# Layer 0's probabilities turned by DMA in 16-bit planes, and a cross pair between layer 1's self pairs

## The chip, the cores and the metric

One core of one Trainium2 chip. The metric is the device time of one execution in microseconds, lower is better; the median of three runs of the kernel before is 4849.32 us (4847.84 to 4849.81).

## What is computed

Four transformer layers in a row over x of 32 batches x 112 tokens x 256 and a context of 32 x 375 x 256. Layers 0 and 2 have cross attention with 16 heads of 64 (layer 0 with 4 key and value heads), layers 1 and 3 self and cross attention with 16 heads of 16. The reference, cut to what matters:

```python
# layer 0: RMS norms, grouped cross attention, x + h @ wo.T
# layer 1: per attention
sim = einsum('bhid,bhjd->bhij', fq(q, dq, 128), fq(k, dk, 128)) * SCALE
attn = softmax(sim)
out = einsum('bhij,bhjd->bhid', fq(attn, dw, 0), fq(v, dv, 128)) @ wo + bo
# then a * gelu(g) @ ff_w2, with a, g the halves of h3 @ ff_w1 + ff_b1
# layer 2: cross attention (h = 16, d = 64) and a relu feed-forward
# layer 3: causal self attention, cross attention, relu feed-forward
```

fq rounds to 8-bit steps; layer 1 therefore holds scores' operands and probabilities exactly in bf16, the other layers compute in f32.

## The kernel before, in words

Two batches make a stream of N = 224 tokens; 16 streams go through each layer, activations transposed (features on partitions). An attention is cut into octets of 8 heads of one batch; two heads (units) make a pair. The order of pairs is written out in `place_attention`: a stream of layer 0 or 2 has 4 cross octets of 4 pairs; in layers 1 and 3 two octets of self pairs (2 pairs each, four heads per unit) stand inside the first two cross octets, after their second pair. So a layer 1 stream has 20 pairs.

A pair goes through: scores on PE into 2 of 4 PSUM banks (`tensor_scores`; scores of a pair wait for the exponentials of the pair two before, and in the layers of `QUADS` two pairs are issued together), max on VectorE (L1698), exp on ScalarE with a running sum (L1563), reciprocal on VectorE (L1705), weighing on GpSimd (L1961 in layer 1, L1964 in the others), into one of 8 slots of `e`. Then the probabilities must be transposed, in one of three ways:

- turn: PE transposes them (`tensor_turn`, L1380, three 112 x 125 chunks a unit) into a PSUM ring, ScalarE or VectorE copy to `probs` (L1603, L1784). Layers 0 and 3, and layer 3's self pairs (L1377).
- layer 1: VectorE writes bf16 steps (L1746), a DMA transpose from SyncE's queue puts them into `probs` (L2001).
- in words, for the layers of `WORDS` (layer 2's cross pairs): the f32 words are split into two planes of 16-bit halves (VectorE L1730 or GpSimd L1946, by pair in turn), SyncE issues a DMA transpose into `planes` (L1996, the flip), and VectorE (L1734) or ScalarE (L1537) merges the halves to f32 in `probs`. There are three slots for halves (`SPLITS`), two for planes (`PLANES`); a flip waits for the merge two pairs before.

The value products (L1411 in layer 0, L1418 in layer 2, L1426 in layer 1, L1401 for self) follow when an octet is turned. All projections (L1437) and norms go through the same ring of 4 PSUM banks as jobs, each with a save by VectorE or ScalarE. Layer 1's gate and up products (h by weights) end in a Gelu on ScalarE (L1531).

`Plan.arrange` lays all steps in a fixed order for each engine beforehand: from the steps' engines, costs and positions it takes for each free engine the ready step of lowest position; steps marked "VA" go to whichever of VectorE and ScalarE is free. The engines then run these orders with semaphores. A changed cost, engine or position so moves instructions everywhere.

```python
WORDS = (2,)
SPLIT_BY = ("V", "G")
QUADS = (0, 2, 3)
self.add("split", p, by, 1.7, p.index + 1.4)
self.add("flip", p, "D", 4.2, p.index + 1.6)
self.add("merge", p, "VA", 1.45, p.index + 2.4)
```

## Time and profile before

| | |
|---|---|
| median of 3 runs | 4849.32 us |
| profiled execution | 4847.86 us, span 4846.1 us |
| PE busy | 4440.9 us, 92% |
| VectorE / ScalarE / GpSimd busy | 2955.7 / 2974.7 / 2282.1 us |
| mean granted TensorE clock | 0.955 |
| layer 0, layer 1, layer 2, layer 3, roughly | to 921, 2216, 3690, 4846 us |

The page cuts the span into 40 slices of 121 us, with a digit for the busy tenths of each engine. Rows of groups give the count, busy time and mean of one instruction. Busy time of back-to-back instructions is counted once where they overlap. A 4-byte matmul shows as two records, a transpose as one.

### The profile page before, as it was taken

How to read it: one execution, taken by the hardware profiler on the slowest of the kernel's cores; microseconds unless marked ns; L12 is line 12 of the kernel's file. 1: busy time of each engine (PE TensorE's matmuls, PEld its weight loads, DVE VectorE, ACT ScalarE, POOL GpSimd, SP SyncE). 2: the span in 40 equal slices, each digit the busy share in tenths (PEclk: the TensorE clock that was granted, in tenths of full speed). 3: DMA queues.
4: the chain of work that ended last, by engine and by line, in shares of the span. 5: the costliest groups of instructions: out<-in, count | busy, mean ns of one | idle time of the engine just before them, and what ended most of it. 6: DMA issues, size and time to landing. Idle time of an engine off the chain costs nothing.

```text
span 4846.1 us, 84907 instructions
## 1 busy us (share of the span) xinstructions
PE 4440.9 (92%) x30496; PEld 3230.0 (67%) x30496; DVE 2955.7 (61%) x6426; ACT 2974.7 (61%) x9009; POOL 2282.1 (47%) x4132
## 2 busy tenths in 40 slices
PE   8999999967787878789999999999999999999998
PEld 5666666646565656566666666666667777778777
DVE  6566566566666666666555555555555666667665
ACT  4555555688888888885444454444445666666664
POOL 3333333465656565664444444444444444444443
PEclk9999999979888888889999999999999999999999
DMA  2000000032333232343433333333332100000000
GB/s 85 21 21 24 21 21 22 25 90 62 62 61 64 61 62 63 61 86 68 98 76 77 75 74 77 77 74 74 77 76 47 41 19 19 18 19 19 18 18 7
DMA packets 631891, 249.53 MB, mean 51 GB/s; under 512 B 596784, under 2 KB 613424, under 8 KB 630064
## 3 DMA queue, kind: packets, MB, share of 16 engines
q1 hardware_dynamic: 631472, 244.10, 23.0%
q8 instruction: 244, 4.00, 0.3%
q14 instruction: 175, 1.43, 0.1%
HBM read 82.53 MB, written 14.68 MB: 20 GB/s over the span
## 4 chain that ended last, share of the span: by engine, by line
PE 82%; ACT 8%; POOL 4%; DVE 3%; issue 2%; DMA 2%; SPq 0%; ACTq 0%; POOLq 0%; DVEq 0%
PE ring L1437 51%; PE score L1366 11%; PE ring L1380 7%; ACT e L1563 5%; PE ring L1418 3%; PE ring L1411 3%; PE ring L1426 2%; DMA probs<-halves 2%; POOL e L1961 1%; POOL e L1964 1%; PE ring L1377 1%; PE ring L1401 1%; ACT work L1624 1%; PE ring L1452 1%; DVE nmax L1698 1%
## 5 line engine op out<-in xcount | busy, mean ns | idle before, releaser
L1964 POOL TENSOR_SCALAR e<-e,rsum 112x375 f32<-112x375 f32 (+1 forms) x2048 | 1102.2, 556 | 1677.4 <-DVE rsum L1705 1642.5
L1698 DVE TENSOR_REDUCE nmax<-score 112x2 f32<-112x750 f32 (+1 forms) x1152 | 1066.4, 951 | 407.0 <-PE score L1366 406.4
L1563 ACT ACTIVATE e<-score,nmax 112x375 f32<-112x375 f32 (+1 forms) x2048 | 1038.6, 537 | 117.8 <-DVE nmax L1698 115.5
L1437 PE MATMUL ring<-h,weights 128*128 128x224 f32 x3840 | 872.1, 369 | 34.5 <-ACT work L1624 24.9
L1437 PEld LDWEIGHTS ring<-h,weights 128*128 128x128 f32 x3840 | 734.3, 197 | 145.1 <-issue 52.7
L1366 PE MATMUL score<-keys,q 64*112 64x375 f32 (+2 forms) x3584 | 607.3, 493 | 235.4 <-ACT e L1563 231.4
L1603 ACT COPY probs<-ring 125x336 f32<-125x336 f32 (+1 forms) x625 | 252.5, 452 | 746.2 <-PE ring L1380 635.4
L1366 PEld LDWEIGHTS score<-keys,q 64*112 64x112 f32 (+2 forms) x3584 | 232.7, 166 | 539.0 <-ACT e L1563 289.5
L1437 PE MATMUL ring<-weights,ctx 128*128 128x512 f32 (+4 forms) x1536 | 587.1, 515 | 0.0
L1437 PE MATMUL ring<-ctx,weights 128*128 128x375 f32 x1536 | 567.2, 491 | 1.0 <-DVE heads L1799 0.8
L1563 ACT ACTIVATE e<-score,nmaxc,quant 112x375 f32<-112x375 f32 (+1 forms) x1024 | 555.1, 554 | 10.7
L1961 POOL TENSOR_SCALAR e<-e,rsumw 112x375 f32<-112x375 f32 (+1 forms) x1024 | 497.2, 505 | 30.3
L1380 PEld LDWEIGHTS ring<-consts,e 112*125 112x125 f32 x3072 | 372.4, 188 | 129.3 <-issue 90.4
L1563 ACT ACTIVATION_READ_ACCUMULATOR e<-score,nmax 112x1 f32 x2048 | 458.1, 224 | 0.0
L1380 PE MATMUL ring<-consts,e 112*125 112x112 f32 x3072 | 415.3, 279 | 5.1 <-POOL e L1964 3.0
L1437 PEld LDWEIGHTS ring<-weights,ctx 128*128 128x128 f32 (+2 forms) x1536 | 306.9, 202 | 143.8 <-issue 96.2
L1437 PE MATMUL ring<-work,weights 128*128 128x224 f32 (+1 forms) x1792 | 398.4, 372 | 1.0 <-DVE work L1827 0.6
L1437 PEld LDWEIGHTS ring<-ctx,weights 128*128 128x128 f32 x1536 | 277.6, 191 | 174.6 <-issue 66.8
L1437 PEld LDWEIGHTS ring<-work,weights 128*128 128x128 f32 x1792 | 335.1, 190 | 38.6 <-issue 12.3
L1850 DVE COPY values<-ring 125x128 f32<-125x128 f32 (+4 forms) x368 | 162.3, 470 | 272.9 <-PE ring L1437 272.0
L1437 PE MATMUL ring<-heads,weights 128*128 128x224 f32 x1536 | 323.0, 359 | 3.6 <-ACT work L1624 1.8
L1437 PEld LDWEIGHTS ring<-heads,weights 128*128 128x128 f32 x1536 | 286.1, 192 | 21.3 <-issue 10.2
(128 smaller groups left out, 5782.1 us busy)
## 6 DMA issues: line engine op xcount, KB each, us to landing
ctx<-ctx_t SPq DMA_DIRECT2D x128, 375.0 KB, 3.1
out_t<-x SPq DMA_DIRECT2D x64, 224.0 KB, 2.0
x<-out_t SPq DMA_DIRECT2D x48, 224.0 KB, 2.6
weights<-weights SPq DMA_DIRECT2D x7, 1024.0 KB, 5.9
probs<-halves SPq DMA_TRANSPOSE x320, 2.7
planes<-halves SPq DMA_TRANSPOSE x256, 3.4
x<-x_t SPq DMA_DIRECT2D x16, 224.0 KB, 2.5
weights<-weights SPq DMA_DIRECT2D x1, 3328.0 KB, 11.5
```

The source lines that it names most:

```text
L1366: ins = pe.matmul(score_bank(u)[0:S, n * width:(n + 1) * width], lhs, rhs, start=not masked, stop=not masked or n == nt - 1)
L1380: ins = pe.transpose(dst[0:R, c * S:(c + 1) * S], src[:, c * R:(c + 1) * R], idt[0:S, 0:S])
L1411: ins = pe.matmul(ps[64 * odd:64 * odd + 64, 0:4 * S], vs[chunk_rows(0, c), c, kv:kv + 64], four_heads(o, c, odd), start=c == 0, stop=c == ...
L1418: ins = pe.matmul(ps[64 * odd:64 * odd + 64, i * S:(i + 1) * S], vs[chunk_rows(2, c), c, hd:hd + 64], probs_of(o, c, 2 * i + odd if plan.i ...
L1426: ins = pe.matmul(ps[32 * p:32 * p + 32, 0:S], vs[chunk_rows(layer, c), c, hd:hd + 32], probs_of(o, c, p + 4 * odd, S), start=c == 0 and o ...
L1437: ins = pe.matmul(out_, a, b_, start=n == 0, stop=n == len(parts) - 1)
L1563: ins = nc.scalar.activation(e_of(u)[:, n * width:(n + 1) * width], score_bank(u)[0:S, n * width:(n + 1) * width], ACT.Exp, bias=minus, sc ...
L1603: ins = nc.scalar.copy(dst, src)
L1698: ins = dve.tensor_reduce(to, src, AX, ALU.max, negate=True)
L1850: ins = dve.tensor_copy(dst, src)
L1961: ins = nc.gpsimd.tensor_scalar(mine, mine, rsumw[0:S, slot(u), n:n + 1], ROUND, ALU.mult, ALU.add)
L1964: ins = nc.gpsimd.tensor_scalar(mine, mine, rsum[0:S, slot(u), n:n + 1], 0.0, ALU.mult, ALU.add)
```

## The change

Cross pairs of layer 0 now go in words as layer 2's: `WORDS = (0, 2)`. The split is made in two instructions per pair, one per half plane: in layer 0 one on GpSimd and one on ScalarE (new for it), in layer 2 both on VectorE or both on GpSimd as before. All merges, of layer 2 too, are VectorE's. Layer 0 leaves `QUADS`: its scores are issued pair by pair. The chunks of layer 0's context become 128, 128 and 119 rows, as in layer 2. In layer 1, of the two self pairs of an octet one stands after the second and one after the third cross pair. Layer 0's output projections get a position one pair later. The slots of `halves` are shared with layer 1's steps by address. Planner costs follow.

```diff
-WORDS = (2,)
-SPLIT_BY = ("V", "G")
+WORDS = (0, 2)
+SPLIT_BY = {0: ("GA",), 2: ("VV", "GG")}
+MERGE_BY = "V"
...
-QUADS = (0, 2, 3)
+QUADS = (2, 3)
...
-                        if beside and n == 1:
+                        if beside and layer == 1:
+                            if n in (1, 2):
+                                self.pair(beside)
+                        elif beside and n == 1:
                             self.pair(beside)
                             self.pair(beside)
...
-        self.row(e + 3.5, e + 4.6, [("o", layer, s, 0, m, "V") for m in range(KC)])
+        late = 1.0 if layer == 0 else 0
+        self.row(e + 3.5 + late, e + 4.6 + late, [("o", layer, s, 0, m, "V") for m in range(KC)])
...
-                by = SPLIT_BY[self.nth_halved[p] % len(SPLIT_BY)]
-                self.add("split", p, by, 1.7, p.index + 1.4)
-                self.add("flip", p, "D", 4.2, p.index + 1.6)
-                self.add("merge", p, "VA", 1.45, p.index + 2.4)
+                by = SPLIT_BY[o_.layer]
+                for h in range(2):
+                    e = by[self.nth_halved[p] % len(by)][h]
+                    self.add("split", (p, h), e, {"G": 0.95, "A": 0.8, "V": 0.6}[e], p.index + 1.4)
+                self.add("flip", p, "D", 3.5, p.index + 1.6)
+                self.add("merge", p, MERGE_BY, 0.9 if MERGE_BY == "V" else 1.2, p.index + 2.4)
...
+                elif kind == "split":
+                    to, src = split(wait, *x_)
+                    nc.scalar.copy(to, src).then_inc(halved["A"], 1)
...
-            return [(to[:, h, :, 0:T], src[:, h, :, :]) for h in range(2)]
+            return to[:, h, :, 0:T], src[:, h, :, :]
```

How instructions move. PE in layer 0, the middle of a stream, before (consts by e are the transposes, heads by weights the output projection, h by weights the queries, work by weights the keys, probs by values the value products):

```order
L1366 MATMUL score<-keys,q 112x375 x4
L1380 MATMUL ring<-consts,e 125x112 x12
L1437 MATMUL ring<-heads,weights 128x224 x16
L1366 MATMUL score<-keys,q 112x375 x4
L1380 MATMUL ring<-consts,e 125x112 x12
L1437 MATMUL ring<-h,weights 128x224 x4
L1437 MATMUL ring<-work,weights 128x375 x2
L1411 MATMUL ring<-probs,values 64x448 x6
L1366 MATMUL score<-keys,q 112x375 x4
L1380 MATMUL ring<-consts,e 125x112 x12
```

and with the change, a like piece:

```order
L1378 MATMUL score<-keys,q 112x375 x2
L1423 MATMUL ring<-probs,values 64x448 x6
L1378 MATMUL score<-keys,q 112x375 x4
L1449 MATMUL ring<-heads,weights 128x224 x16
L1378 MATMUL score<-keys,q 112x375 x2
L1423 MATMUL ring<-probs,values 64x448 x6
L1378 MATMUL score<-keys,q 112x375 x2
L1449 MATMUL ring<-work,weights 128x375 x2
L1378 MATMUL score<-keys,q 112x375 x2
L1449 MATMUL ring<-h,weights 128x224 x2
L1378 MATMUL score<-keys,q 112x375 x2
```

The transposes are gone, and each pair's scores stand alone with other work between most of them.

ScalarE in layer 0, before (probs from ring are turn copies, e from score the exponentials):

```order
L1603 COPY probs<-ring 125x3x112 x3
L1563 ACTIVATE e,sums<-score,nmax 112x375 x4
L1603 COPY probs<-ring 125x3x112 x2
L1563 ACTIVATE e,sums<-score,nmax 112x375 x4
L1664 COPY keys<-ring 128x375
L1603 COPY probs<-ring 125x3x112 x2
L1563 ACTIVATE e,sums<-score,nmax 112x375 x4
```

and now:

```order
L1549 COPY halves<-e 112x2x375 x2
L1664 ACTIVATE q<-ring 128x224
L1578 ACTIVATE e,sums<-score,nmax 112x375 x2
L1664 ACTIVATE q<-ring 128x224
L1578 ACTIVATE e,sums<-score,nmax 112x375 x2
L1549 COPY halves<-e 112x2x375
L1664 ACTIVATE q<-ring 128x224
L1578 ACTIVATE e,sums<-score,nmax 112x375 x4
L1549 COPY halves<-e 112x2x375 x2
L1664 ACTIVATE q<-ring 128x224
L1549 COPY halves<-e 112x2x375
L1664 ACTIVATE q<-ring 128x224
```

Copies to halves have taken the place of turn copies, and queries' saves have come over from VectorE.

PE in layer 1 around the second self octet, before (keys alone 112x112 are self scores, keys with q cross scores, probs by own the self values):

```order
L1366 MATMUL score<-keys 112x112 x8
L1437 MATMUL ring<-squares,mean_w 128x224 x4
L1401 MATMUL ring<-probs,own 32x112 x16
L1366 MATMUL score<-keys 112x112 x8
L1366 MATMUL score<-keys,q 112x375 x6
L1437 MATMUL ring<-h,weights 128x224 x4
L1426 MATMUL ring<-probs,values 32x112 x24
L1437 MATMUL ring<-h,weights 128x224 x12
```

and now:

```order
L1378 MATMUL score<-keys 112x112 x8
L1378 MATMUL score<-keys,q 112x375 x2
L1413 MATMUL ring<-probs,own 32x112 x16
L1449 MATMUL ring<-h,weights 128x224 x4
L1438 MATMUL ring<-probs,values 32x112 x24
L1449 MATMUL ring<-h,weights 128x224 x8
L1378 MATMUL score<-keys 112x112 x8
L1449 MATMUL ring<-h,weights 128x224 x4
L1378 MATMUL score<-keys,q 112x375 x2
L1449 MATMUL ring<-h,weights 128x224 x8
L1378 MATMUL score<-keys,q 112x375 x2
```

Where two self pairs were followed by three pairs of cross scores, one cross pair and 12 of the h by weights products stand between the self pairs, and 4 and 8 more between the following scores.

## Rows read from the trace of the kernel before

**Rows 1.** The page's slices: busy tenths in 40 equal parts of the span.

```profile
PE   8999999967787878789999999999999999999998
...
ACT  4555555688888888885444454444445666666664
...
PEclk9999999979888888889999999999999999999999
```

**Rows 2.** Windows: stretch, PE, PEld, DVE, ACT, POOL busy us (instructions), clock, DMA share, GB/s.

```profile
443.90:501.60 57.70, 57.32 (x320) 38.76 (x319) 34.63 (x72) 31.00 (x94) 21.75 (x35) 1.00 0.08 22
...
1487.50:1566.70 79.20, 59.31 (x401) 46.00 (x400) 48.84 (x112) 67.22 (x200) 47.78 (x99) 0.87 0.30 62
...
2371.00:2462.50 91.50, 91.50 (x524) 61.09 (x523) 51.86 (x101) 43.83 (x106) 38.37 (x52) 1.00 0.38 77
...
3760.00:3960.00 200.00, 191.14 (x1893) 155.46 (x1886) 138.76 (x331) 127.63 (x480) 91.66 (x197) 0.97 0.10 32
```

**Rows 3.** Instructions of line 1531, the Gelu of layer 1 (min/median/max ns, first and last start).

```profile
L1531 ACT ACTIVATE heads<-heads x16: 1696/1697/1698, 1092.8 to 2280.6; 128x1792 f32<-128x1792 f32 x16
```

**Rows 4.** The chain of waits, 400 to 520 us (layer 0): start us, us, what.

```profile
442.14 1.49 PE ring L1380 x12
...
443.64 6.07 PE ring L1437 x32
...
499.84 1.49 PE ring L1380 x12
```

**Rows 5.** Groups by line, 200 to 900 us: count | busy us, mean ns | idle before.

```profile
L1603 ACT COPY probs<-ring 125x336 f32<-125x336 f32 x219 | 84.6, 443 | 285.3 <-PE ring L1380 284.0
...
L1784 DVE COPY probs<-ring 125x336 f32<-125x336 f32 x172 | 79.5, 497 | 0.0
```

**Rows 6.** Groups by line, 2300 to 3600 us (layer 2).

```profile
L1964 POOL TENSOR_SCALAR e<-e,rsum 112x375 f32<-112x375 f32 x460 | 297.4, 658 | 584.5 <-DVE rsum L1705 584.5
...
L1946 POOL TENSOR_SCALAR halves<-e 112x750 uint16<-112x750 uint16 x230 | 194.7, 864 | 10.1
...
L1537 ACT COPY probs<-planes 128x1344 uint16<-128x1344 uint16 x115 | 168.1, 1462 | 164.2 <-DMA planes<-halves 164.2
...
L1734 DVE COPY probs<-planes 128x1344 uint16<-128x1344 uint16 x115 | 97.9, 852 | 12.0 <-DMA planes<-halves 11.9
```

**Rows 7.** Tile planes, whole span: ns min/median/max of issues; landing times.

```profile
L1996 SPq DMA_TRANSPOSE planes<-halves x256: 1260/1361/3815, 2225.9 to 3687.1; - x128
...
DMA to landing us min/median/max: 3.4/3.4/8.1
```

**Rows 8.** PE's timeline in layer 1: start us, us, what, [idle before <-releaser].

```profile
1230.18 0.41 PE L1366 MATMUL score<-keys 32*112 32x112 bf16 x8
1234.55 0.56 PE L1366 MATMUL score<-keys,q 32*112 32x375 bf16 x2 [3.95 <-ACT e L1563]
1239.04 0.56 PE L1366 MATMUL score<-keys,q 32*112 32x375 bf16 x2 [3.93 <-ACT e L1563]
...
1241.87 3.33 PE L1437 MATMUL ring<-h,weights 128*128 128x224 f32 x8 [0.66 <-ACT work L1624]
```

**Rows 9.** Windows of 4 us in layer 1.

```profile
1232.00:1236.00 4.00, 0.56 (x2) 0.17 (x2) 1.88 (x5) 3.97 (x18) 1.81 (x5) 0.50 0.00 0
...
1264.00:1268.00 4.00, 4.00 (x23) 3.55 (x22) 2.25 (x6) 2.30 (x5) 2.31 (x5) 1.00 0.28 56
```

**Rows 10.** Groups by line, 1000 to 2200 us, ScalarE.

```profile
L1637 ACT ACTIVATE heads<-ring,vectors 128x224 f32<-128x224 f32 x69 | 30.9, 448 | 50.4 <-PE ring L1437 50.4
...
L1593 ACT ACTIVATE own<-work,minus_magic 112x128 bf16<-112x128 f32 x28 | 9.5, 390 | 0.0
```

**Rows 11.** Tiles rsum (200 to 900 us) and e (2300 to 3600): ns min/median/max.

```profile
L1964 POOL TENSOR_SCALAR e<-e,rsum x388: 591/595/732, 201.8 to 895.2; 112x375 f32<-112x375 f32 x194
...
L1964 POOL TENSOR_SCALAR e<-e,rsum x460: 587/594/1257, 2302.3 to 3597.9; 112x375 f32<-112x375 f32 x154
...
L1730 DVE COPY halves<-e x230: 531/546/1180, 2304.8 to 3595.0; 112x750 uint16<-112x750 uint16 x115
```

More of the change, by code:

```diff
@@ L231, in place_attention @@
         self.nth_halved = {p: i for i, p in enumerate(self.halved)}
-        self.ones = [p for p in self.pairs if p.octet.layer == 1]
-        self.nth_of_one = {p: i for i, p in enumerate(self.ones)}
+        self.turned = [p for p in self.pairs if p.octet.layer == 1 or self.in_words(p.octet)]
+        self.nth_turned = {p: i for i, p in enumerate(self.turned)}
+        self.nth_of_one = {p: i for i, p in enumerate(p for p in self.pairs if p.octet.layer == 1)}
         for p in self.pairs:
@@ L243, in halves_before, with place_of @@
     def halves_before(self, p):
-        i = self.nth_halved[p]
-        found = [self.halved[i - SPLITS]] if i >= SPLITS else []
-        if p in [h for h in self.halved if h.octet.layer > 1][:SPLITS]:
-            found = found + self.ones[-STEPSLOTS:]
-        return found
-    def steps_before(self, p):
-        i = self.nth_of_one[p]
-        if i >= STEPSLOTS:
-            return [self.ones[i - STEPSLOTS]]
-        return [h for h in self.halved if h.octet.layer == 0][-SPLITS:]
+        a, z = self.place_of(p)
+        i = self.nth_turned[p]
+        return [o for o in self.turned[max(0, i - 6):i] if self.place_of(o)[0] < z and a < self.place_of(o)[1]]
+    def place_of(self, p):
+        if p.octet.layer == 1:
+            at = self.nth_of_one[p] % STEPSLOTS * 8 * P
+            return at, at + 8 * P
+        at = self.nth_halved[p] % SPLITS * 4 * CHUNKS * P
+        return at, at + 4 * CHUNKS * P
     def in_words(self, o):
@@ L512, in before @@
                 elif self.in_words(self.pairs[x.index - ES // 2].octet):
-                    yield "split", self.pairs[x.index - ES // 2]
+                    for h in range(2):
+                        yield "split", (self.pairs[x.index - ES // 2], h)
                 else:
@@ L518, in before @@
             yield "weigh", x
-            for p in self.steps_before(x):
+            for p in self.halves_before(x):
                 yield "flip", p
         elif kind == "split":
-            yield "weigh", x
-            for p in self.halves_before(x):
+            yield "weigh", x[0]
+            for p in self.halves_before(x[0]):
                 yield "flip", p
@@ L529, in before @@
         elif kind == "flip" and self.in_words(x.octet):
-            yield "split", x
+            for h in range(2):
+                yield "split", (x, h)
             i = self.nth_halved[x]
@@ L1130, in merged_of, with split @@
             return part(probs[:, o.index % 2, :], 0, [8 * CHUNKS, S])[:, at:at + 2 * CHUNKS, :]
-        def split(eng, wait, p):
+        def split(wait, p, h):
             wait.wait_ge(weighed, nth["weigh", p])
@@ L1137, in split, with split_done @@
             src = e[0:S, pair_slots(p), 0:T].bitcast(U16).rearrange("p a (n h) -> p h a n", h=2)
-            return [(to[:, h, :, 0:T], src[:, h, :, :]) for h in range(2)]
+            return to[:, h, :, 0:T], src[:, h, :, :]
+        def split_done(wait, p):
+            for h in range(2):
+                wait.wait_ge(halved[plan.split_by[p, h]], nth["split", (p, h)])
         def merge(wait, p):
@@ L1550, in scalar_exp @@
                 elif plan.in_words(before.octet):
-                    wait.wait_ge(halved[plan.split_by[before]], nth["split", before])
+                    split_done(wait, before)
                 else:
@@ L1728, in vector_program @@
                 elif kind == "split":
-                    for to, src in split(dve, wait, x_):
-                        ins = dve.tensor_copy(to, src)
-                    ins.then_inc(halved["V"], 1)
+                    to, src = split(wait, *x_)
+                    dve.tensor_copy(to, src).then_inc(halved["V"], 1)
                 elif kind == "merge":
@@ L1737, in vector_program @@
                     wait.wait_ge(weighed, nth["weigh", p])
-                    for before in plan.steps_before(p):
+                    for before in plan.halves_before(p):
                         flip_done(wait, before)
@@ L1904, in pool_program @@
             nc.gpsimd.memset(minus_magic[:, :], -ROUND).then_inc(consts_made, 1)
[L1905 removed]
+            nc.gpsimd.memset(halves[:, :], 0).then_inc(consts_made, 1)
             nc.gpsimd.memset(own[:, :, :], 0.0).then_inc(zeroed, 1)
@@ L1944, in pool_program @@
                 if kind == "split":
-                    for to, src in split(pool, wait, x_):
-                        ins = nc.gpsimd.tensor_scalar(to, src, 1.0, 0.0, ALU.mult, ALU.add)
-                    ins.then_inc(halved["G"], 1)
+                    to, src = split(wait, *x_)
+                    nc.gpsimd.tensor_scalar(to, src, 1.0, 0.0, ALU.mult, ALU.add).then_inc(halved["G"], 1)
                     continue
@@ L1990, in sync_program @@
                     if plan.in_words(p.octet):
-                        wait.wait_ge(halved[plan.split_by[p]], nth["split", p])
+                        split_done(wait, p)
                         i = plan.nth_halved[p]
```

15 lines of the change are left out of this document (7 added, 8 removed).

## The prediction

> **What bounds the kernel now.** I read the slices of the page first. TensorE (PE) is at nine tenths or more in layers 0, 2 and 3 and at seven to eight in the stretch between, where ScalarE (ACT) is at eight and the granted clock is lower; that stretch is layer 1 [rows 1]. The table of windows then gives one stream's period in each layer. In layer 0 PE is busy 57.32 of 57.70 us, ScalarE 31.0, VectorE 34.6, GpSimd 21.75: PE alone is the bound. In layer 1 ScalarE is busiest, 67.2 of 79.2 us, and PE 59.3 at a mean clock of 0.87. In layer 2 PE is busy without a gap, in layer 3 191.1 of 200 us, 95.6% [rows 2]. The Gelu passes, one a stream, lie 1092.8 to 2280.6 us apart for 15 periods, 79.2 us each [rows 3]. The chain of waits of layer 0 repeats after 57.70 us (442.14 to 499.84) and runs through PE. It holds eight groups of turns a stream, 12 transposes in 1.49 us each [rows 4].
>
> **Layer 0, PE.** The change removes the turns of layer 0 from PE: 8 x 1.49 = 11.9 us a stream. Scores, value products and projections stay: a pair's scores are half of a quad's. Without a gap PE needs 57.3 - 11.9 = 45.4 us a stream.
>
> **Layer 0, the others.** ScalarE loses its turn copies (84.6 us in 700 us, or 12.13 periods: 7.0 a stream) and VectorE its own (79.5 us: 6.6) [rows 5]. Each of the 16 pairs now needs one half split by GpSimd, one by ScalarE, a flip and a merge by VectorE. Layer 2 has these operations: a half on GpSimd takes 0.864 us, a merge on VectorE 0.851, a merge of 1344 elements on ScalarE 1.462 [rows 6]. A half on ScalarE is not in the trace. It is a copy of 750 elements on the engine that copies 1344 in 1.462 us, so 0.82 us by elements; the ends are 0.55 (VectorE's median for the same half [rows 11]) and 1.46. I take 0.82, the same engine's. Queries' saves move too, some 4 a stream from VectorE to ScalarE at 0.38 us. The sums: ScalarE 31.0 - 7.0 + 13.1 + 1.6 = 38.7 us (34.4 to 49 by the ends), VectorE 34.6 - 6.6 + 13.6 - 1.6 = 40.0, GpSimd 21.75 + 13.8 = 35.6, against PE's 45.4. PE stays the longest, but VectorE is close behind, and every score waits for the exponentials two pairs before it, in an order fixed beforehand; GpSimd, ScalarE, SyncE and VectorE now stand in line between a probability and its product. So PE won't be without gaps. The nearest rows are layer 3, where the busiest engine fills 95.6%, and layer 1, where it fills 85% [rows 2]: 47.5 or 53.4 us a stream. The others are fuller than in layer 3 (where VectorE is at 69%) but PE leads, as there: I take 93%, 48.8 us. Gain 57.7 - 48.8 = 8.9 us. The first and last of 16 streams overlap with start and with layer 1, so I count 15.5: **138 us**. Ends: 45.4 us (190 us gained) and 53.6 (64).
>
> Queued on SyncE are 16 flips a stream, each taking 1.36 us of its queue and landing 3.4 us after issue in the median [rows 7]: 21.8 us of 48.8; the loads and stores besides are few. A flip waits for the merge two pairs before, and behind it wait the loads of context and x; those are asked for streams ahead, so I cost this at nothing. Without that cover a context load would hold VectorE's scaling and then the key products. The two-plane loop costs 3.4 + 0.85 and two hand-overs of 0.1, 4.45 us for two pairs, against 48.8 / 8 = 6.1 available: no cost.
>
> **Layer 1.** Here the change adds and removes no instruction; it moves one cross pair between the two self pairs, and with it the saves and PE's order. Before, PE issues the second self pair's scores at 1230.18, then three cross pairs' scores with nothing between; the first two wait 3.95 and 3.93 us for exponentials, and the hidden layer's 24 gate products (h by weights) follow only from 1241.87 [rows 8]. While that lasts the granted clock is 0.50, and afterwards PE is filled, as in 1264 to 1268, 4.00 of 4 us, with ScalarE at 2.30 [rows 9]. In the new order 24 of those matmuls stand between the self pairs and the cross scores. At full clock one such product takes 0.38 us (16 in 6.07 [rows 4]), so that is 9.1 us of PE work, moved from a stretch where PE bounds to one where ScalarE does. The planner also moves saves off ScalarE: 39 gate saves at 0.448 us, 28 clips of own values at 0.39 [rows 10], and by the order some 22 clips of cross values and 26 saves of heads that I price at 0.39 too: 47 us, less 2 for clips that come back, 45 us or 2.8 a stream, onto VectorE, which has room (48.8 of 79.2). ScalarE's floor becomes 67.2 - 2.8 = 64.4 us. Its idle time is 12.0 us a stream now. Bounds: all goes (64.4, 14.8 us a stream), nothing but a little (30 us in the layer). Some idle stays, since the start and end of each chain (Gelu, the flips) aren't touched: I keep 7.6 of 12.0, a period of 72.0, which is 89% filled, between layer 1's 85 and layer 3's 96. Gain 7.2 x 15.5 = **112 us**.
>
> **Layers 2 and 3.** All merges of layer 2 go to VectorE: 126 x 1.462 us leave ScalarE, 126 x 0.851 join VectorE, 6.7 us a stream on top of 51.9 of 91.5. PE is busy 91.5 of 91.5 there [rows 2], so both are hidden: zero, within 5 us. If VectorE came late, value products would be next. Layer 3 is untouched. The first pairs of layer 2 wait for flips of layer 1's last slots as before.
>
> **Sum.** The profiled execution took 4847.86 us (span 4846.1), 1.5 below the median of the runs, 4849.32. 4847.9 - 138 - 112 = **4598 us**, 5.2% faster. A difference under 0.2% (10 us) can't be told from none.
>
> **Rivals.**
> Forecast, both gains: 0.60.
> A: layer 1 keeps its period, because ScalarE's waits only move (PE's chain through Gelu, the normalisations and the flips sets the end); 25 us are left there. For it: ScalarE is already 85% filled. Against: the PE gap of rows 8 is 9 us and its work is moved into it. 4848 - 138 - 25 = 4685 us. 0.17.
> B: in layer 0 a second engine takes the bound through contention. In layer 2 GpSimd's weighing has a median of 594 ns, a mean of 658 and a maximum of 1257, more than twice the median [rows 6, 11], where VectorE copies halves and planes; in layer 0 its maximum is 732 [rows 11]. If each of 16 merges held GpSimd for its whole 0.85 us, GpSimd would need 35.6 + 13.6 = 49.2 us, more than PE's 45.4, and at 93% 52.9: gain 4.8 x 15.5 = 74, total 4848 - 74 - 112 = 4662 us. A lower clock in PE's new gaps gives nearly the same: 45.4 / 0.85 = 53.4. Against: layer 2's excess of 64 ns a weighing adds only 2 us a stream. 0.15. The Trainium skill ("SBUF — State Buffer", Who interferes with whom) says VectorE in a two-port mode and GpSimd share one port pair under an exclusive lock, the later one blocked for the whole instruction; the maximum of 1257 ns agrees. By that rule alone the time would be this rival's.
> C: slower. The loop through two planes becomes the bound: issue, landing, merge, then the flip after next. The change puts 16 flips into each layer 0 stream; DMA share says a flip takes 0.38 x 91.5 - 0.08 x 57.7 = 30.2 us for 16, 1.9 us of all engines each [rows 2], so the engines would be (30.2 + 4.6) / 48.8 = 71% busy. With landings of 8.1 us, the longest seen [rows 7], the loop is 8.1 + 0.85 + 0.2 = 9.15 us per two pairs, 73.2 us a stream: +240 - 112, 4976 us. It decides from 8.1 us a loop, where it eats layer 1's gain too (57.7 / 8 = 7.2, and 112 / 15.5 / 8 = 0.9 more). Against: the median landing is the minimum. 0.05.
> D: no change: pair scores, which wait for ScalarE after each pair and not after two, stall PE 0.75 us sixteen times a stream, which is all of 11.9, and layer 1 gains nothing: 4848 us. For it: such waits exist in layer 1 [rows 8]. Against: layer 0 has only cross pairs, and in the new order other work stands between most scores. 0.03.
>
> **Numbers.** The forecast is the likeliest. The range leaves out C, D and the far ends: low 4848 - 190 - 158 (layer 1 at 69 us) = 4500; high 4740, beyond A and B with some of both. Faster 0.92, within 0.2% 0.03, slower 0.05.
>
> **What would show it.** A layer 0 period of 47 to 50 us by the chain, PE 93% busy, clock above 0.95, no transposes there; half copies near 0.82 us on ScalarE; flips landing at 3.4 to 4 us; GpSimd's weighing under 0.7 us. In layer 1 a Gelu spacing of 70 to 74 us, clock above 0.9, no row of three cross scores each waiting near 4 us. Layer 2 at 91.5 us. It would be wrong if ScalarE or the planes' loop, not PE, led in layer 0, or if Gelu spacing stayed at 79.

## The result, and the profile after

The changed kernel takes 4817.94 us (median of 4 runs, 4813.21 to 4819.38) against 4849.57 (4847.84 to 4851.34) for the kernel before, measured beside it: ratio 0.9932, with an interval of 0.9921 to 0.9944. It is 32 us faster where 250 were forecast, outside the range of 4500 to 4740. Its slices on the page, as [rows 1] were for before:

```profile
PE   7999999777878787879999999999999999999998
...
ACT  5777667778777777784333333333344666666664
POOL 6888777666565655553444444444444444444443
PEclk9999999878888888889999999999999999999999
```

After the first slice PE still stands at 9 in layer 0, now with GpSimd beside it at 7 or 8, and the stretch at seven and eight tenths, layer 1, is no shorter and has a lower clock. The next table gives windows, with the columns of [rows 2]: one period of layer 0 (two starts of like scores, one stream apart), 500 us of layer 0, layer 1, and one period of layer 2.

```profile
443.90:497.80 53.90, 50.98 (x222) 28.63 (x219) 39.45 (x66) 38.01 (x95) 41.46 (x51) 0.97 0.66 130
300.00:800.00 500.00, 471.45 (x2070) 257.54 (x2069) 384.04 (x647) 352.95 (x896) 401.22 (x473) 0.98 0.64 126
1080.00:2190.00 1110.00, 881.86 (x5449) 650.90 (x5450) 704.30 (x1642) 868.15 (x2578) 648.88 (x1349) 0.84 0.31 63
2371.00:2462.50 91.50, 91.50 (x509) 60.87 (x509) 61.52 (x110) 29.72 (x90) 41.02 (x55) 1.00 0.38 74
```

Layer 0's period went from 57.7 to 53.9 us, not to 48.8. PE is busy 471.45 of 500 us, 94%, near the 93% of the forecast; but one stream takes 50.98 us of its busy time, where 45.4 had been forecast. Layer 2's period is unchanged, 91.5 of 91.5, and its merges are hidden as forecast. Layer 1 is told by two lines of ScalarE's: nmaxc, which is made for each pair of layer 1 alone and so marks where that layer begins and ends, and the Gelu [rows 3]. First before, then after:

```profile
L1557 ACT ACTIVATE nmaxc<-nmax,quant x320: 281/292/328, 921.3 to 2216.1; 112x2 f32<-112x2 f32 x128, 112x8 f32<-112x8 f32 x32
```

```profile
L1572 ACT ACTIVATE nmaxc<-nmax,quant x320: 281/298/323, 866.9 to 2190.5; 112x2 f32<-112x2 f32 x98, 112x8 f32<-112x8 f32 x62
L1543 ACT ACTIVATE heads<-heads x16: 1696/1697/1698, 1041.5 to 2255.2; 128x1792 f32<-128x1792 f32 x16
```

Layer 1 begins 54.4 us earlier (921.3 to 866.9). It lasts 1323.6 us instead of 1294.8, 28.8 longer, and what follows it 2.9 less. That is the whole difference of the spans of the two profiled executions: -54.4 + 28.8 - 2.9 = -28.5 (4846.1 to 4817.6). The Gelu spacing rose from 79.2 to (2255.2 - 1041.5) / 15 = 80.9 us. So two questions are open: why layer 0 gave 54 us of 138, and why layer 1 lost 29 where it was to win 112.

The groups of layer 0 in the changed kernel, by line and form, 300 to 800 us, columns as in [rows 6]:

```profile
L1977 POOL TENSOR_SCALAR e<-e,rsum 112x375 f32<-112x375 f32 x297 | 220.3, 754 | 86.6 <-DVE rsum L1720 86.3
...
L1960 POOL TENSOR_SCALAR halves<-e 112x750 uint16<-112x750 uint16 x149 | 158.3, 1066 | 9.1
L1748 DVE COPY probs<-planes 128x1344 uint16<-128x1344 uint16 x149 | 146.2, 982 | 44.9 <-DMA planes<-halves 44.8
...
L1378 PE MATMUL score<-keys,q 64*112 64x375 f32 x594 | 134.1, 530 | 15.4 <-ACT e L1578 15.0
L1549 ACT COPY halves<-e 112x750 uint16<-112x750 uint16 x149 | 121.7, 818 | 80.4 <-POOL e L1977 78.4
L1449 PE MATMUL ring<-h,weights 128*128 128x224 f32 x292 | 71.2, 371 | 0.0
```

and the same two groups of PE before:

```profile
L1366 PE MATMUL score<-keys,q 64*112 64x375 f32 x556 | 105.6, 497 | 3.4 <-ACT e L1563 3.4
...
L1437 PE MATMUL ring<-h,weights 128*128 128x224 f32 x271 | 58.6, 354 | 0.0
```

ScalarE's half takes 818 ns (0.82 forecast). VectorE's merge and GpSimd's half and weighing all have a longer mean than in layer 2 [rows 6]. And the same score matmuls keep PE busy 134.1 / 594 = 226 ns a record, where it was 105.6 / 556 = 190; the queries' (h by weights) 244 where it was 216.

In layer 1 the timeline of PE shows two long waits a stream; these are two of the 1310 to 1396 us stretch (start us, us, what, and in brackets the wait and what ended it), and below them the waits of 1080 to 2190 us (waiter, releaser: us, times, longest), some 13.7 periods:

```profile
1327.79 0.56 PE L1378 MATMUL score<-keys,q 32*112 32x375 bf16 x2 [4.06 <-ACT q L1597]
...
1372.76 1.08 PE L1449 MATMUL ring<-h,weights 128*128 128x224 f32 x4 [4.08 <-DVE work L1848]
```

```profile
PE ring L1449 <- DVE work L1848: 53.3, 14, 4.1
...
PE score L1378 <- ACT q L1597: 52.8, 13, 4.1
```

The first cross scores of a stream wait 4.06 us for ScalarE's save of their queries (L1597); before the change such waits summed to 0.9 us in 1180 us. The hidden layer's products wait as long for VectorE's saves of up products (L1848), which multiply with the Gelu's result and so stand behind it; before the change VectorE's saves (L1834) held these products for 1.4 us in the whole 1110.

These waits are not the whole of the loss. The window of 1180 to 2080 us before the change:

```profile
1180.00:2080.00 900.00, 684.32 (x4541) 532.87 (x4540) 549.58 (x1260) 753.01 (x2235) 540.83 (x1119) 0.85 0.32 62
```

By streams of 79.2 us PE was busy 60.2 and idle 19.0. In the changed kernel (712.41 busy, 80.9 a stream) it is busy 64.0 and idle 16.9. So the moved cross pair did cut PE's waiting, and its waits for exponentials fell from 155.9 to 70.3 us in this window; what grew is the time of the same products. PE's timeline shows where: the first line below ends just before the 4.08 us wait, the second begins 4 us after it.

```profile
1364.95 3.29 PE L1449 MATMUL ring<-h,weights 128*128 128x224 f32 x16
1376.98 4.22 PE L1449 MATMUL ring<-h,weights 128*128 128x224 f32 x12
```

A record takes 0.21 us before and 0.35 after; the granted clock is 1.00 from 1362 to 1370 us, 0.50 from 1374 to 1378 and 0.70 from 1378 to 1382. After the wait for the queries it is 0.50 (1326 to 1330) and 0.67 (1330 to 1334). Before the change the half clock fell in part on stretches in which PE had next to nothing to do [rows 9].

### The profile page after: what moved, and what is told of

Same layout as the page of the kernel before. It is cut to its first block, busy times and chain, and to the rows that moved or that the text cites. A ratio compares the mean times of both kernels' runs of the same rounds, so it can differ in the third digit from the quotient of the medians.

```text
span 4817.6 us, 83128 instructions
## 1 busy us (share of the span) xinstructions
PE 4393.7 (91%) x28960; PEld 3065.0 (64%) x28960; DVE 3253.3 (68%) x6694; ACT 2840.1 (59%) x8741; POOL 2644.0 (55%) x4388
## 4 chain that ended last, share of the span: by engine, by line
PE 67%; POOL 13%; ACT 8%; issue 5%; DVE 4%; DMA 2%; SPq 0%; POOLq 0%; ACTq 0%; DVEq 0%
PE ring L1449 45%; PE score L1378 8%; POOL e L1977 6%; ACT e L1578 4%; PE ring L1392 4%; PE ring L1430 3%; POOL halves L1960 3%; PE ring L1438 2%; POOL e L1974 2%; DMA planes<-halves 1%; PE ring L1389 1%; PE ring L1413 1%; DVE probs L1748 1%; DVE nmax L1713 1%; ACT work L1639 1%
## 5 line engine op out<-in xcount | busy, mean ns | idle before, releaser
L1977 POOL TENSOR_SCALAR e<-e,rsum 112x375 f32<-112x375 f32 (+1 forms) x2048 | 1205.8, 605 | 1261.7 <-DVE rsum L1720 1228.6
L1578 ACT ACTIVATE e<-score,nmax 112x375 f32<-112x375 f32 (+1 forms) x2048 | 1038.4, 534 | 380.5 <-DVE nmax L1713 379.1
L1449 PE MATMUL ring<-h,weights 128*128 128x224 f32 x3840 | 926.4, 383 | 74.7 <-DVE work L1848 57.1
L1378 PE MATMUL score<-keys,q 64*112 64x375 f32 (+2 forms) x3584 | 652.0, 504 | 205.0 <-ACT e L1578 145.6
L1449 PE MATMUL ring<-ctx,weights 128*128 128x375 f32 x1536 | 591.8, 509 | 3.0 <-ACT work L1639 2.3
L1748 DVE COPY probs<-planes 128x1344 uint16<-128x1344 uint16 x512 | 480.9, 940 | 142.6 <-DMA planes<-halves 136.6
L1449 PE MATMUL ring<-weights,ctx 128*128 128x512 f32 (+4 forms) x1536 | 560.6, 495 | 0.0
L1960 POOL TENSOR_SCALAR halves<-e 112x750 uint16<-112x750 uint16 x512 | 489.7, 966 | 28.6 <-DMA planes<-halves 1.0
L1449 PE MATMUL ring<-work,weights 128*128 128x224 f32 (+1 forms) x1792 | 409.2, 378 | 11.9 <-DVE work L1740 10.9
L1618 ACT COPY probs<-ring 125x336 f32<-125x336 f32 (+1 forms) x340 | 141.9, 459 | 375.4 <-PE ring L1392 268.5
L1864 DVE COPY values<-ring 125x128 f32<-125x128 f32 (+3 forms) x405 | 187.4, 489 | 256.6 <-PE ring L1449 256.2
L1967 POOL TENSOR_SCALAR rsumw<-rsum,quant 112x2 f32<-112x2 f32 (+1 forms) x320 | 133.4, 417 | 394.2 <-DVE rsum L1720 387.3
```

The lines of the kernel that those rows point to most:

```text
L1378: ins = pe.matmul(score_bank(u)[0:S, n * width:(n + 1) * width], lhs, rhs, start=not masked, stop=not masked or n == nt - 1)
L1449: ins = pe.matmul(out_, a, b_, start=n == 0, stop=n == len(parts) - 1)
L1578: ins = nc.scalar.activation(e_of(u)[:, n * width:(n + 1) * width], score_bank(u)[0:S, n * width:(n + 1) * width], ACT.Exp, bias=minus, sc ...
L1618: ins = nc.scalar.copy(dst, src)
L1748: dve.tensor_copy(to, src).then_inc(merged["V"], 1)
L1864: ins = dve.tensor_copy(dst, src)
```

## The experiments

Ratios are to the kernel before, run on the same chip beside them, with the 95% interval. In the diffs - is the kernel that the text names, + the experiment; they are cut to the lines that matter.

### Each half of the change alone

e1 keeps all of the change but layer 1's order; e2 is the kernel before with layer 1's order alone.

```diff
 e1, from the changed kernel
-                        if beside and layer == 1:
-                            if n in (1, 2):
-                                self.pair(beside)
-                        elif beside and n == 1:
+                        if beside and n == 1:
```

> The changed kernel, but with layer 1's two self pairs together again, as before. Theory (layer 0 gives some 54 us, layer 1's new order costs 25 to 29): about 4790 us, Gelu spacing back at 79.2 us, layer 0 as in the changed kernel (layer 1 begins near 867 us). Rival (layer 1 is slower for its other changes: the saves moved to VectorE, the shared slots): 4815 to 4820 us, Gelu spacing 80.9.

> The kernel before, with only the new places of layer 1's self pairs. Theory (the new order by itself costs, because up products, held by the Gelu, block the ring and the first cross scores wait for their queries' clip): 4870 to 4880 us, Gelu spacing 80.9 us. Rival (the order itself is harmless or helps): 4849 us or less.

e1: 4799.05 us, ratio 0.9897 (0.9882 to 0.9912), 50 us faster than before; layer 1 begins at 863.8 and has the Gelu 79.5 us apart (1038.4 to 2231.6), so the rest of the change costs layer 1 little. e2: 4874.35, ratio 1.0049 (1.0034 to 1.0064), 25 us slower, with the Gelu 81.0 us apart (1094.7 to 2310.3). -50 + 25 = -25, and the whole change gives -32, so the halves nearly add up. The order of layer 1 is by itself a loss, and e2's PE has the same two waits, in 1080 to 2190 us: 52.6 us for ScalarE's queries and 57.2 us for VectorE's up saves.

### Layer 1: which of the two waits costs

The positions of the steps between a stream's self and its cross attention are counted from `z`, the position of its last self pair (`a, z = self.span(layer, "self", s)`). With the new order that last self pair comes one pair later, and with it output projection, norm and queries of the cross attention; the cross pairs that need those queries do not move. e9 takes one from `z`; e8 leaves `z` and moves up products and second feed-forward product one pair later, so that they are issued when the Gelu is done.

```diff
 e9, from e2
+        z -= layer == 1
         self.row(z + 4.0, z + 4.5, [("o"
 e8, from e2
-        self.row(e + 12.5, e + 15.5, [("up"
+        self.row(e + 13.5, e + 16.5, [("up"
-        self.row(e + 16.5, e + 17.5, [("f2"
+        self.row(e + 17.5, e + 18.5, [("f2"
```

> As e2, but what follows layer 1's self attention (output projection, norm, queries of the cross attention) keeps its old place, which the later second self pair had pushed back by one pair. Theory (the first cross pair now waits for its queries' clip, 52.8 us of PE waiting in layer 1 of the changed kernel, 3.8 us a stream): 20 to 50 us below e2's 4874. Rival (the queries are late whatever their place, since ScalarE and GpSimd are full): within 8 us of e2.

> As e2, but layer 1's up products (and the last product after them) get a position one pair later, so that fewer of them wait in the ring for the Gelu. Theory (PE's wait for the saves of up products, 111 us in layer 1 of the changed kernel, is new and on its path): 15 to 50 us below e2's 4874. Rival (another wait takes its place): within 8 us of e2.

e9: 4764.59 us, ratio 0.9827 (0.981 to 0.9843), 110 below e2 and 84 below before. e8: 4832.95, 0.9968 (0.9956 to 0.998), 41 below e2. The Gelu in e9:

```profile
L1535 ACT ACTIVATE heads<-heads x16: 1696/1697/1698, 1088.9 to 2198.3; 128x1792 f32<-128x1792 f32 x16
```

73.96 us apart, inside the 70 to 74 of the forecast. Windows of 1180 to 2080 us, first of the changed kernel, then of e2, then of e9:

```profile
1180.00:2080.00 900.00, 712.41 (x4392) 527.89 (x4392) 566.64 (x1338) 701.59 (x2089) 526.85 (x1102) 0.83 0.31 61
```

```profile
1180.00:2080.00 900.00, 718.85 (x4400) 533.07 (x4400) 564.16 (x1340) 700.08 (x2091) 524.69 (x1100) 0.82 0.30 61
```

```profile
1180.00:2080.00 900.00, 737.22 (x4890) 560.84 (x4889) 618.45 (x1463) 779.08 (x2340) 579.04 (x1221) 0.92 0.34 70
```

ScalarE's busy time is 779.08 / 900 x 73.96 = 64.0 us a stream in e9 and 701.59 / 900 x 80.9 = 63.1 in the changed kernel, where the floor was forecast as 64.4: the saves did move much as read from the order. The queries' wait of about 4 us a stream is gone in e9. Of the 7.1 us a stream between e2 and e9, PE's idle time gives 2.9 (16.3 to 13.4) and its busy time 4.1, from 718.85 / 900 x 81.0 = 64.7 to 737.22 / 900 x 73.96 = 60.6 us, with the granted clock up from 0.82 to 0.92. The busy time is the larger part: with one long wait less, fewer products follow one at half clock. The waits for VectorE's up saves stay: 56.3 us in 1080 to 2190. Two waits of one length stood in the table; taking away the one gave 110 us with the other still there.

e8 has neither of the two, by the waits of 1180 to 2080 us, but others in their place. First e2, then e8:

```profile
PE score L1369 <- ACT e L1566: 69.8, 54, 2.4
PE ring L1440 <- DVE work L1837: 44.7, 11, 4.1
PE score L1369 <- ACT q L1585: 44.5, 11, 4.1
```

```profile
PE score L1369 <- ACT e L1566: 142.8, 68, 5.7
PE score L1369 <- DVE own L1777: 38.0, 12, 3.2
```

PE's waits for exponentials doubled, and waits for the self pairs' operands (own) are new. With the Gelu 78.3 us apart PE is idle 18.2 us a stream, for 16.3 in e2, and busy 60.0 for 64.7, at a clock of 0.91. So e8 lost on waits and won 41 us by faster products alone.

e10 and e11 try both on the whole change.

```diff
 e10, from the changed kernel
+        z -= layer == 1
 e11, from e10
-        self.row(e + 12.5, e + 15.5, [("up"
+        self.row(e + 13.5, e + 16.5, [("up"
-        self.row(e + 16.5, e + 17.5, [("f2"
+        self.row(e + 17.5, e + 18.5, [("f2"
```

> The changed kernel, with what follows layer 1's self attention at its old place, as in e9. Theory (the two halves of the change are nearly independent; the order of layer 1 gains some 84 us once its queries aren't pushed back, layer 0 some 50): 4700 to 4730 us, Gelu spacing near 74. Rival (the gain of e9 needs the rest of the kernel before): above 4760.

> As e10, with the up products one pair later too, as in e8. Theory (PE's wait behind the Gelu, 99 us in 900 of e9, is still on the path): 20 to 50 us below e10. Rival (with the queries in time, ScalarE, 87% busy, sets the pace): within 10 us of e10.

e10: 4723.34 us, ratio 0.974 (0.9724 to 0.9756), 95 below the changed kernel, Gelu 74.2 us apart. e11: 4830.7, 0.9962 (0.9947 to 0.9977): 107 us worse than e10, Gelu 81.9, clock 0.82. The expectation that the two gains add was wrong. By streams e11's PE is idle 17.7 us and busy 64.2, e10's 13.4 and 60.8 at a clock of 0.91. Waits of e11 in 1180 to 2080 us, then of e10:

```profile
PE score L1379 <- ACT e L1579: 122.3, 66, 3.1
DVE x L1828 <- PE ring L1450: 102.6, 66, 4.1
...
PE ring L1450 <- DVE work L1849: 46.9, 11, 4.3
```

```profile
PE score L1379 <- ACT e L1579: 85.4, 83, 3.1
...
PE ring L1450 <- DVE work L1849: 48.0, 12, 4.3
...
DVE x L1828 <- PE ring L1450: 40.4, 25, 2.3
```

The wait that the later up products were to remove, L1450 for L1849, is still there (46.9 for 48.0), and VectorE now waits 102.6 us for the products that end in x. Where the chain through x bites was not separated further; it stays open why the same edit won 41 us on e2 and lost 107 on e10.

### Layer 0: PE's own work, or the others?

e7 is the kernel before with one edit, its layer 0 scores issued pair by pair. e5 is e1 with layer 0's scores back by quads, the planes staying.

```diff
 e7, from before
-QUADS = (0, 2, 3)
+QUADS = (2, 3)
 e5, from e1
-QUADS = (2, 3)
+QUADS = (0, 2, 3)
```

> The kernel before, but layer 0's scores are issued pair by pair; nothing else. Theory (small groups cost PE time): layer 0's period rises by 2 to 4 us, the total to 4880 to 4910 us, though PE has the same instructions. Rival (pair scores cost PE nothing): 4849 us, within 5.

> As e1, but layer 0's scores are issued for two pairs together again. Theory (in the changed layer 0 PE does some 50.4 us of work a stream, not 45.4, because small groups cost more: a pair's scores take 0.82 us from start to start against 1.45 for two, and the groups between them more too): PE's busy time per score record falls from 226 towards 190 ns, the period by 2 to 3 us a stream, the total by 30 to 45 us against e1, to about 4760. Rival (the long line of GpSimd, ScalarE, flip and merge sets the pace, and pair scores are there to keep it fed): no gain or slower than e1, PE with longer idle times before scores.

e7: 4919.96 us, ratio 1.0147 (1.0132 to 1.0162): issuing pairs costs 71 us with the same instructions. Group and window of 300 to 800 us, for 105.6 us x556 and 496.56 busy before:

```profile
L1366 PE MATMUL score<-keys,q 64*112 64x375 f32 x516 | 114.2, 523 | 10.4 <-ACT e L1563 10.1
```

```profile
300.00:800.00 500.00, 484.91 (x2556) 306.52 (x2552) 282.96 (x557) 255.43 (x767) 175.28 (x280) 0.99 0.07 21
```

With 64 score records a stream the window holds 516 / 64 = 8.06 streams, a period of 62.0 us. PE is busy 484.91 / 8.06 = 60.1 us of it, for 57.2 before (496.56 over 556 / 64 = 8.69): 3 us a stream are more busy time, and 1.5 are waits. A window counts busy time where records overlap once, so the 3 us are no artefact of overlapping groups; the groups' own busy times overlap with their neighbours' and can't be added. The timelines show where it lies. A quad before, with the turns behind it, and then the changed kernel:

```profile
440.63 1.52 PE L1366 MATMUL score<-keys,q 64*112 64x375 f32 x8
442.07 1.56 PE L1380 MATMUL ring<-consts,e 112*125 112x112 f32 x12
```

```profile
404.38 0.89 PE L1378 MATMUL score<-keys,q 64*112 64x375 f32 x4
405.20 1.53 PE L1449 MATMUL ring<-work,weights 128*128 128x375 f32 x4
406.66 0.89 PE L1378 MATMUL score<-keys,q 64*112 64x375 f32 x4
...
426.81 1.02 PE L1449 MATMUL ring<-h,weights 128*128 128x224 f32 x4
427.77 0.89 PE L1378 MATMUL score<-keys,q 64*112 64x375 f32 x4
```

From the start of a quad's scores to that of the next work it is 1.44 us, 0.18 a record; of a pair's 0.82 (404.38 to 405.20), 0.205. The same holds of what stands between: two queries' products, four records, take 0.96 us (426.81 to 427.77), 0.24 a record, where 32 in a row took 6.07 [rows 4], 0.19 each. Counted so over PE's timelines of 300 to 780 us, each group up to the start of the next and without idle time, a score record takes 180 ns before and 207 in e7, a queries' record 192 and 213.

e5: 4888.02 us, ratio 1.0083 (1.0068 to 1.0099), 89 above e1. A score record falls to 110.1 / 544 = 202 ns, but PE is busy 421.07 of 500 us only. My expectation of a gain was wrong, and its rival came. The largest of its waits:

```profile
PE score L1375 <- ACT e L1575: 41.8, 20, 3.0
PE ring L1420 <- DVE probs L1745: 22.9, 23, 3.1
```

By 64 score records a stream e5's PE is busy 49.5 us and idle 9.3, e1's 50.7 and 2.6 (475.51 busy, 600 records). Grouping scores gives PE 1.2 us back and takes more in waits. Why is not shown; as I read it, four scores at once need all score banks free and hand VectorE, ScalarE and GpSimd two pairs at a time, with a path of four engines behind each. e12 groups the other side, the queries' products between the scores, in twos.

```diff
 e12, from e1
-        self.row(c - 10.7 + early, c - 1.3, [("q", layer, s, 0, m, "VA") for m in range(8)])
+        if layer == 0:
+            for m in range(8):
+                self.job(c - 7.7 + 6.4 * (m // 2) / 3, "q", layer, s, 0, m, "VA")
+        else:
+            self.row(c - 10.7 + early, c - 1.3, [("q", layer, s, 0, m, "VA") for m in range(8)])
```

> As e1, but layer 0's query projections have their positions in twos, so that more of them stand together on PE. Theory (each small group between scores costs PE 0.1 to 0.2 us): 5 to 20 us below e1. Rival (the grouping is not what costs, or longer groups hold up the scores as the quads do): no gain or slower.

e12: 4802.48 us, 0.9902 (0.9887 to 0.9917), 3 above e1: no gain. The new positions joined only some of the queries: in 300 to 800 us PE's timeline has 17 groups of eight records where e1 has 9, and 39 of four where e1 has 56. PE's busy time did fall, 469.51 for 475.51 us at the same 600 score records, and its value products waited longer for merges, 14.0 for 5.4 us. As in e5, what grouping gave was lost in waits.

### Layer 0: GpSimd, VectorE and their meeting

e3 gives both halves of every second pair to ScalarE; e4 gives both halves to GpSimd and the merges of layer 0 to ScalarE, so that VectorE makes no plane copies there at all.

```diff
 e3, from e1
-SPLIT_BY = {0: ("GA",), 2: ("VV", "GG")}
+SPLIT_BY = {0: ("GA", "AA"), 2: ("VV", "GG")}
 e4, from e1
-SPLIT_BY = {0: ("GA",), 2: ("VV", "GG")}
+SPLIT_BY = {0: ("GG",), 2: ("VV", "GG")}
-                self.add("merge", p, MERGE_BY, 0.9 if MERGE_BY == "V" else 1.2, p.index + 2.4)
+                self.add("merge", p, "A" if o_.layer == 0 else MERGE_BY, 1.45 if o_.layer == 0 else 0.9, p.index + 2.4)
```

> As e1, but in layer 0 every second pair has both halves copied by ScalarE, so that GpSimd does 8 halves a stream and not 16. Theory (in layer 0 GpSimd, stretched by the port it shares with VectorE, sets the pace): GpSimd is relieved of 8.5 us a stream, ScalarE goes to about 45; layer 0's period falls from 54 to 51 or 52, total 20 to 45 us below e1. Rival (the fixed order and the pair scores set the pace, not GpSimd): within 10 us of e1 or slower.

> As e1, but in layer 0 all merges are ScalarE's and both halves GpSimd's, so VectorE makes no 16-bit plane copies there. Theory (plane copies by VectorE stretch GpSimd's instructions): GpSimd's weighing falls from a mean of 754 to about 595 ns and its halves from 1066 to about 831, so that GpSimd with 16 more halves a stream needs 49 us, not 61, and the period is 52 to 56. Rival (GpSimd's long means have another cause, such as DMA traffic): the means stay at 750 and 1060, GpSimd needs 60 us and the total is 80 us or more above e1.

e3: 4833.05 us, 0.9969 (0.9957 to 0.998), 34 above e1, though GpSimd's busy time fell from 405.60 to 305.44 of 500 us. ScalarE had the halves instead, so this does not show that GpSimd's load costs nothing: e14 below takes the same load off GpSimd (308.43 us busy) and gives it to nobody, and gains 26 us. e3 shows that ScalarE is no better place for them. e4: 4871.86, 1.0048 (1.0032 to 1.0065), 73 above e1. ScalarE merges in 1462 ns and GpSimd holds twice the halves, with 399.18 and 421.00 of 500 us busy; no run separates the two. But its durations answer another question. GpSimd in e4, 300 to 800 us:

```profile
L1957 POOL TENSOR_SCALAR halves<-e 112x750 uint16<-112x750 uint16 x280 | 235.5, 864 | 2.1
...
L1974 POOL TENSOR_SCALAR e<-e,rsum 112x375 f32<-112x375 f32 x282 | 166.6, 604 | 66.0 <-DVE rsum L1717 65.6
```

The weighing is back at 604 ns from 754 and the half at 864, the value of layer 2 [rows 6], from 1066. The flips still run in e4, so it is VectorE's plane copies that lengthen GpSimd's work; e13 below, where they are short, agrees. The Trainium skill ("SBUF — State Buffer", Who interferes with whom) says that VectorE in a two-port mode and GpSimd take turns under an exclusive lock; the trace agrees in kind, the longest weighing of the changed kernel's 300 to 800 us being 2746 ns at a median of 594.

What it costs in time takes a kernel in which the rest stays. In e13 the merges of layer 0, from the 33rd pair on, copy 32 of 1344 half words (the rest of `probs` stays stale); in e14 GpSimd's halves copy 16 of 375 columns; e15 does both.

```diff
 e13, from e1
+                    if x_.octet.layer == 0 and plan.nth_halved[x_] >= 32:
+                        to, src = to[:, 0:16, :], src[:, 0:16, :]
                     dve.tensor_copy(to, src).then_inc(merged["V"], 1)
 e14, from e1
+                    if x_[0].octet.layer == 0 and plan.nth_halved[x_[0]] >= 32:
+                        to, src = to[:, :, 0:16], src[:, :, 0:16]
                     nc.gpsimd.tensor_scalar(to, src, 1.0, 0.0, ALU.mult, ALU.add).then_inc(halved["G"], 1)
```

> As e1, but layer 0's merges, from its 33rd pair on, copy 16 columns of 672 and leave the rest of the probabilities stale: VectorE does no plane copies to speak of, the waits and the order stay. Theory 1 (PE's work in small groups, 50.4 us a stream, is the floor): period 51 to 53 us, 15 to 45 us below e1. Theory 2 (the port that VectorE's merges and GpSimd share costs the missing time): period 47 to 50, 60 to 105 us below e1, GpSimd's weighing back at 595 ns.

> As e1, but GpSimd's halves in layer 0, from its 33rd pair on, copy 16 columns of 375 and leave the low halves of the words stale: GpSimd is relieved of 17 us a stream, VectorE's merges stay whole. Theory 1 (PE's floor): 15 to 45 us below e1. Theory 2 (GpSimd, stretched, is the bound): 60 us or more below e1. Rival to both (neither; merges and flips hold the line): within 10 us of e1.

> As e1 with both e13's and e14's cuts. Nothing but PE is then near full in layer 0. Theory 1: period 50.4 to 51.5, 35 to 55 us below e1, PE busy 98% or more, a score record still 220 to 235 ns. Theory 2 (PE's records are long only because PE waits for late engines): the score record falls to 190 to 200 ns and the period to 46 to 48, over 90 us below e1.

| 300 to 800 us | e1 | e13 | e14 | e15 |
|---|---|---|---|---|
| median, us | 4799.05 | 4752.67 | 4773.31 | 4746.32 |
| ratio | 0.9897 | 0.9796 (0.9779 to 0.9814) | 0.9843 (0.9827 to 0.9859) | 0.9786 (0.977 to 0.9801) |
| against e1 | | -46 | -26 | -53 |
| PE busy of 500 us | 475.51 | 491.94 | 484.61 | 492.31 |
| weighing, mean ns | 744 | 635 | 728 | 631 |

e15's window and its scores:

```profile
300.00:800.00 500.00, 492.31 (x2208) 273.55 (x2208) 290.23 (x683) 369.39 (x946) 252.76 (x501) 0.99 0.70 133
```

```profile
L1375 PE MATMUL score<-keys,q 64*112 64x375 f32 x630 | 140.6, 526 | 4.9 <-ACT e L1575 4.7
```

This is the floor of PE in this order. Its clock is 0.99, nothing else holds it, and a score record still takes 140.6 / 630 = 223 ns. By the 157 merges of the window, 9.81 streams, the period is 51.0 and PE's busy time 492.31 / 9.81 = 50.2 us. VectorE's merges and GpSimd's halves together cost 53 us on top of that in e1. Taken away alone, the merges give 46 of them and the halves 26, so the two are no sum. Both cuts take away the engines' plain work along with their meeting, so 53 us is the most that the meeting can cost, and its own share is not shown.

### Costs for the planner, and the best version

e6 tells the planner what layer 0's steps really take; e16 adds that to e10.

```diff
 e6, from e1
-                self.add("weigh", p, "G", (2.7 if own else 1.15)
+                self.add("weigh", p, "G", (2.7 if own else 1.5 if o_.layer == 0 else 1.15)
-                    {"G": 0.95, "A": 0.8, "V": 0.6}[e]
+                    {"G": 1.1 if o_.layer == 0 else 0.95, "A": 0.82, "V": 0.6}[e]
-                    0.9 if MERGE_BY == "V"
+                    (1.0 if o_.layer == 0 else 0.9) if MERGE_BY == "V"
```

> As e1, but the planner takes for layer 0 the durations that the changed kernel's profile shows (weighing 1.5 us a pair, a GpSimd half 1.1, a merge 1.0). The work is the same, the order another. Theory (PE's own work in small groups is the floor, 50.4 of some 53.9 us): within 15 us of e1's 4799. Rival (the order, laid out for durations that GpSimd and VectorE don't keep, is what costs the missing 80 us): 30 us or more below e1.

> e10 with e6's planner costs for layer 0, both gains together: 4723 less 5 to 15, so 4708 to 4718. Rival (the orders interact): 4723 or more.

e6: 4790.71 us, 0.9875 (0.986 to 0.989), 8 below e1, about what can be told from nothing. e16: 4708.0 us, 0.971 (0.9692 to 0.9727). It beats the kernel before by 143 us and the changed one by 110. Of the 110, layer 1 gives 101: nmaxc runs from 854.2 to 2076.7, 1222.5 us for 1323.6. Its window of 1180 to 2080 us:

```profile
1180.00:2080.00 900.00, 734.90 (x4860) 557.25 (x4862) 614.29 (x1442) 770.93 (x2294) 565.42 (x1191) 0.92 0.33 70
```

## Why the prediction was wrong, step by step

**Faster: right**, at 0.92, but by an eighth of the forecast. Each of the two large terms fell short for a reason of its own.

**"Without a gap PE needs 45.4 us a stream": this step failed in layer 0.** The turns went, as said, and PE remained the bound, 94% filled for 93 forecast. The term that was mis-sized is PE's work: 50.98 us in one period, 50.2 at its floor in e15. "A pair's scores are half of a quad's" was counted by instructions. e7 shows that cutting quads into pairs alone costs 3 us of busy time and 1.5 us of waits a stream. Where the 4.8 us (50.2 - 45.4) lie is read from the timelines, each group up to the start of the next, the kernel before against e15: scores 180 to 208 ns a record, x64, is 1.8 us; queries 192 to 222, x32, 1.0; keys' products (work by weights) 324 to 341, x16, 0.3; value products 200 to 204, x48, 0.2. The rest, some 1.5 us, is spread over small groups and not accounted for, and no run separates these parts from each other. 12 us of turns so bought 5 us of slower matmuls.

**Rival B, contention: right in kind, smaller in size.** It was to give a period of 52.9 by GpSimd as the bound. GpSimd is not the bound: it is busy 401.22 of 500 us where PE is busy 471.45. But e13 to e15 say that merges and halves at full length cost 26 us (halves), 46 (merges) or 53 (both), the last some 3 us a stream, about PE's idle 28.55 of 500 us in the changed kernel. The rival added 16 x 0.85 = 13.6 us to GpSimd's stream. The means over the medians show 32 x (754 - 594) ns + 16 x (1066 - 832) ns = 8.9 us, and GpSimd's busy time is 401.22 us over 594 / 64 = 9.28 streams, 43.2 a stream, not 49.2. So two thirds of the time that full blocking would take was taken, but on an engine with 10 us to spare. The forecast's sign that weighing stays under 0.7 us was wrong: 754 ns.

The layer 0 account: 45.4 forecast, + 4.8 PE's work in small groups, + some 3 waits with these engines, is 53.2, against 53.9 read. (57.7 - 53.9) x 15.5 = 59 us, and layer 1 begins 54 earlier. The 8.9 us a stream of the forecast were 3.8.

**"It moves one cross pair between the two self pairs": this step failed in layer 1.** The term was worked out from the pairs and left out what is positioned from them. `z` carried output projection, norm and queries one pair later, and the first cross scores waited for the queries. In the excerpts of the order this was not to be seen, since it is a distance between a step and its user and no sequence. In its place the runs showed 4.1 us of waiting for the queries a stream and, behind it, products at half clock: putting `z` back gave 7.1 us a stream, 110 us from e2 to e9. The forecast had priced the moved products at full clock, and expected a mean clock above 0.9; it was 0.83. The mechanism that I forecast is real: with `z` put back the spacing is 73.96 and 74.2 us (72.0 forecast), ScalarE's work 64.0 (64.4), and e9 gains 84 us alone for the 112 forecast. Rival A was nearer, with a gain of 25 us left in layer 1, but there was a loss of 29, and its reason was another: waits did not only move, new ones came. The forecast's own sign of being wrong, a Gelu spacing that stays at 79, was met with 80.9. Its other sign was a row of three cross scores each waiting near 4 us; what came was one such wait a stream, for queries and not for exponentials.

**The small terms held.** Halves on ScalarE 818 ns for 0.82. Layer 2 at 91.5 of 91.5 us with all merges on VectorE. No stall from the planes, rival C: over the whole span 512 flips, 3.5 us from issue to landing in the median and 5.6 at the longest. Rival C was priced with landings of 8.1 and decided from a loop of 8.1, which is landings of some 7 us.

```profile
planes<-halves SPq DMA_TRANSPOSE x512, 3.5
```

**Rival D** was half right: pair scores do stall and slow PE, by 4.3 us a stream (e7), not by all of 11.9.

## What to carry to other kernels

Count changes of group on a full TensorE, not only its matmuls: the same products in groups half as long took 3 us a stream more of PE's time here, so work removed from it may come back as shorter groups. When an item is moved in an order written by positions, look for every position that is counted from it, and check for each the distance to its first user. And where two engines slow each other, shrink one side's work in a kernel of its own before giving the slowdown a price: GpSimd's durations rose by a quarter, and the time by about 1% at most.

## What was unexpected of the hardware

A score record of 64 rows by 375 columns kept PE busy 190 ns in quads and 226 in pairs. Two products of the 128-row kind took 0.96 us when they stood alone between scores, 0.24 a record, and 0.19 in a row of 32. In layer 1 the mean granted clock was 0.82 with two 4 us waits a stream (e2) and 0.92 with one (e9), and PE's busy time for the same work 64.7 and 60.6 us: the period fell by 7.1 us with a wait of 4.1 taken away. The mean clock alone does not tell the price, though: before the change it was 0.85 and the busy time 60.2, since there the half clock fell in part on stretches with little work. And a slowdown of a quarter on GpSimd's two commonest instructions, which I had not expected to be so large and so cheap at once, took about 1% of the time at most.
